# Expert results of a two-layer decoder: from gathers by slot to scatters by row number

## The reference

```python
scores = xf @ Wg
w, idx = jax.lax.top_k(scores, K)            # K = 2 of E = 8 experts
w = jax.nn.softmax(w, axis=-1)
xhat = (xf - mu) * jax.lax.rsqrt(var + EPS)
normed = xhat[None] * gamma[:, None] + beta[:, None]
h = jax.nn.relu(jnp.einsum('end,edf->enf', normed, W1) + b1[:, None])
out = jnp.einsum('enf,efd->end', h, W2) + b2[:, None] + xf[None]
cw = jnp.sum(w[..., None] * jax.nn.one_hot(idx, E, dtype=w.dtype), axis=1)
y = jnp.einsum('ne,end->nd', cw, out)
```

## Time and profile before

| | |
|---|---|
| device time, median of 3 runs | 2757.27 us (2757.04 to 2762.21) |
| the profiled execution's own time | 2763.08 us |
| its span, first to last instruction | 2761.8 us |
| granted TensorE clock, mean over the span | 0.895 |
| PE busy | 2188.1 us, 79% |
| DVE, ACT, POOL busy | 1627.2, 1182.3, 617.8 us |
| scatters ahead of the loop | 748.1 to 791.6 us |
| loop over slots, PE | 795.8 to 1084.4 us |
| from there to the linear attention | 1084.4 to 1146.4 us |
| transfers issued by POOL | 8.39 MB, 0.9% of 16 engines |

### The profile page before, as it was taken

The page is one execution under the profiler, slowest core; times in us unless marked ns, Lnnn a source line. Parts: engine busy times, 40 slices in busy tenths (PEclk is TensorE's granted clock), DMA queues, the critical chain, the costliest instruction groups (busy, mean ns, idle before and its releaser), DMA issues. The chain is left out here.

```text
span 2761.8 us, 41898 instructions
## 1 busy us (share of the span) xinstructions
PE 2188.1 (79%) x15624; PEld 1422.4 (52%) x15694; DVE 1627.2 (59%) x3375; ACT 1182.3 (43%) x2185; POOL 617.8 (22%) x541
## 2 busy tenths in 40 slices
PE   5987589896439997487789999994877786878678
PEld 3554167573427886244345565562555443455534
DVE  5866955467823333566666666625777533777663
ACT  2133845455113332132235555553665433566442
POOL 2110013132153554201110000002221222222152
PEclk9997799897669998688989999996998998899999
DMA  4113124341431111333411101102000001000100
GB/s 136 46 53 92 40 85 143 118 136 47 204 120 40 47 47 51 88 79 79 122 32 33 29 25 37 25 1 91 1 1 1 11 1 61 1 1 1 41 8 24
DMA packets 103780, 151.80 MB, mean 55 GB/s; under 512 B 25188, under 2 KB 84544, under 8 KB 101056
## 3 DMA queue, kind: packets, MB, share of 16 engines
q1 hardware_dynamic: 100512, 140.73, 16.5%
q0 software_dynamic: 3072, 8.39, 0.9%
HBM read 107.07 MB, written 47.98 MB: 56 GB/s over the span
## 5 line engine op out<-in xcount | busy, mean ns | idle before, releaser
L2688 DVE TENSOR_REDUCE xa_max<-psum 128x1 f32<-128x1024 f32 (+1 forms) x256 | 248.4, 988 | 132.5 <-PE psum L2598 131.9
L2769 ACT ACTIVATE xa_work<-psum 128x1024 f32<-128x1024 f32 (+1 forms) x208 | 212.9, 1024 | 188.9 <-PE psum L2621 187.1
L2636 PE MATMUL psum<-xa_work,xa_values 128*33 128x128 f32 (+1 forms) x3328 | 223.9, 277 | 0.0
L2636 PEld LDWEIGHTS psum<-xa_work,xa_values 128*33 128x33 f32 (+1 forms) x3328 | 168.1, 111 | 73.7 <-issue 70.2
L2959 PE MATMUL psum<-wqkv_l,x_hl_l 128*128 128x512 bf16 x538 | 136.9, 400 | 66.2 <-POOL x_hl_l L3219 33.2
L3325 PE MATMUL psum<-h_ch_f,w_f 128*128 128x512 bf16 (+1 forms) x556 | 136.6, 400 | 34.4 <-issue 13.1
L1838 DVE TENSOR_SCALAR moe_raw<-psum,tile_b 128x256 f32<-128x256 f32 x184 | 78.3, 475 | 137.2 <-PE psum L1673 136.1
L994 POOL TENSOR_TENSOR text_q<-text_q 128x512 bf16<-128x512 f32 x64 | 81.8, 1293 | 344.8 <-ACT text_q L1364 344.6
L1919 POOL TENSOR_TENSOR x_ch<-moe_raw,x_ch 128x512 bf16<-128x512 f32 x92 | 105.6, 1158 | 147.1 <-ACT x_ch L1883 145.1
L1673 PE MATMUL psum<-moe_rows,moe_w 128*128 128x256 bf16 x1104 | 131.7, 277 | 3.0 <-POOL moe_rows L1915 3.0
L2621 PE MATMUL psum<-xa_query_rows,xa_key_rows 98*128 98x512 bf16 (+1 forms) x416 | 127.2, 388 | 8.4 <-ACT xa_work L2769 7.7
(11 more groups left out here) (457 smaller groups left out, 4763.5 us busy)
## 6 DMA issues: line engine op xcount, KB each, us to landing
text_q<-in_moe_w SPq DMA_DIRECT2D x64, 256.0 KB, 3.8
experts<-text_q SPq DMA_DIRECT2D x64, 256.0 KB, 3.0
moe_w<-experts SPq DMA_DIRECT2D x16, 1024.0 KB
xa_key_rows<-cross_keys SPq DMA_DIRECT2D x48, 200.1 KB, 3.4
ctx_chunk<-in_ctxT SPq DMA_DIRECT2D x24, 300.0 KB, 3.0
moe_rows<-slots_in SPq DMA_DIRECT2D x23, 256.0 KB, 2.8
slots_out<-moe_rows SPq DMA_DIRECT2D x23, 256.0 KB, 2.2
cross_keys<-xa_k_hl SPq DMA_DIRECT2D x6, 800.5 KB, 3.7
```

What stands on the lines that cost most here:

```text
L2636: ins = pe.matmul(total.ap[a * LANE:a * LANE + VC, c:c + PIECE], t["v"][b][0:rows, kt, first + a, :], exps[0:rows, a, c:c + PIECE], start= ...
L2688: v.tensor_reduce(t["maxes"][n % 2][:, qt * HU + a, part:part + 1], u.wide[:, 0:c1 - c0], AX.X, ALU.max).then_inc(*u.free)
L2769: act.activation(t["exps"][k % EXPS][0:rows], u.wide[0:rows].rearrange("p (m q) -> p m q", q=T), ACT.Exp, scale=1.0 / float(np.sqrt(np.flo ...
```

## The change

Each row of `slots_in` gets a 257th word, an integer: the row of `pairs_out` to which this row's result belongs (k x 2048 + token for a pair, numbers from 4096 on for unused rows). DVE writes it into the tiles before the first 16 scatters (k = 0), and anew, once these have landed, for the other 16 (k = 1); the scatters go in the order k, then tile. The fill now writes zero rows out of on-chip memory and, with a second transfer, 5888 single words. The store of each slot on SP is gone; in its place POOL issues two indirect transfers a slot (`send`), which take `y_out` to `pairs_out` by the numbers that lie in the slot's `x_in` buffer. The load into that buffer therefore also waits for this slot's two sends. Behind the loop, SP loads the results with 8 plain transfers of 512 KB in place of POOL's 32 gathers, and DVE waits once for each pair number and group in place of once for each instruction. Each added wait stands in the diff, cut to its core:

```diff
@@ -1541,11 +1543,19 @@
-def fill_slots(m):
...
-    for a in range(0, SLOTS * SLOT, NTOK):
-        n = min(NTOK, SLOTS * SLOT - a)
-        m.nc.sync.dma_start(m.dram["slots_in"][a:a + n, :], m.dram["x"][0:n, :]).then_inc(*m.slots.filled.up(16))
+def fill_slots(m, s, blank, number):
...
+    g, n = m.nc.gpsimd, SLOTS * SLOT // P
+    g.memset(blank[:], 0.0).then_inc(*s.blank.up())
+    g.tensor_scalar(number[:, 0, :], m.const("ramp")[:, 0:n], float(P), float(PAIRS * NTOK + P - 1), ALU.mult, ALU.add).then_inc(*s.blank.up())
+    g.wait_ge(*s.blank(2))
+    g.tensor_tensor(number[:, 0, :], number[:, 0, :], m.const("left").to_broadcast([P, n]), ALU.subtract).then_inc(*s.blank.up())
+    g.wait_ge(*s.blank(3))
+    g.tensor_copy(number[:, 1, :].bitcast(INT), number[:, 0, :]).then_inc(*s.blank.up())
+    slots = m.dram["slots_in"].rearrange("(n p) c -> p n c", p=P)
+    m.nc.sync.wait_ge(*s.blank(4))
+    m.nc.sync.dma_start(slots[:, :, 0:D], blank[:].unsqueeze(1).to_broadcast([P, n, D])).then_inc(*m.slots.filled.up(16))
+    m.nc.sync.dma_start(slots[:, :, D:ROW], number[:, 1, :].unsqueeze(2), allow_slow_non_contiguous=True).then_inc(*m.slots.filled.up(16))
@@ -1557,25 +1567,26 @@
-                 slot=sb("pair_slot", [P, PAIRS, TILES]), slot_i=sb("pair_slot_i", [P, PAIRS, TILES], mybir.dt.int32),
+                 slot=sb("pair_slot", [P, PAIRS, TILES]), nth=sb("token_number", [P, TILES]), slot_i=sb("pair_slot_i", [P, PAIRS, TILES], mybir.dt.int32),
...
-        raw, rows = sb("moe_raw", [P, 2 * 1024]), sb("moe_rows", [P, TILES, D])
+        raw, rows = sb("moe_raw", [P, 2 * 1024]), sb("moe_rows", [P, TILES, ROW])
...
-        t.update(hat=rows, value=[quarter(raw[:], n) for n in range(2)], act=[quarter(raw[:], 2 + n) for n in range(2)],
-                 x_in=[quarter(flat_rows, n) for n in range(3)], y_out=[quarter(flat_rows, 3 + n) for n in range(2)],
-                 gates=flat_rows[0:NE, 5 * BANK:6 * BANK],
-                 x=[flat_rows[:, (6 + n) * BANK:(7 + n) * BANK].bitcast(BF16).rearrange("p (x h c) -> p x h c", x=2, h=HALVES)
+        t.update(hat=rows[:, :, 0:D], number=rows[:, :, D:ROW].rearrange("p t c -> p (t c)").bitcast(INT), sent=rows, value=[quarter(raw[:], n) for n in range(2)], act=[quarter(raw[:], 2 + n) for n in range(2)],
+                 y_out=[quarter(flat_rows[:, 0:8 * BANK], n) for n in range(2)],
+                 x_in=[flat_rows[:, 5 * BANK + 2 * ROW * n:5 * BANK + 2 * ROW * (n + 1)].rearrange("p (a c) -> p a c", c=ROW) for n in range(3)],
+                 gates=flat_rows[0:NE, 4 * BANK:5 * BANK],
+                 x=[flat_rows[:, (2 + n) * BANK:(3 + n) * BANK].bitcast(BF16).rearrange("p (x h c) -> p x h c", x=2, h=HALVES)
...
-                      "in_high in_low h_high h_low stored0 stored1 combined")
-        moved = m.signals("scattered back0 back1 back2 back3 back4 back5 back6 back7", first=70)
+                      "in_high in_low h_high h_low combined")
+        moved = m.signals("scattered0 scattered1 scattered2 scattered3 sent0 sent1 numbered back0 back1 back2 back3", first=70)
@@ -1614,23 +1629,28 @@
         sp.dma_start(t["w2"][:, e], dram["experts_2"][e]).then_inc(*s.w_loaded.up(16))
 
     slots_in = dram["slots_in"].rearrange("(j a p) d -> j p a d", a=2, p=P)
-    slots_out = dram["slots_out"].rearrange("(j a p) d -> j p a d", a=2, p=P)
 
     def load(j):
         if j > 2:
             sp.wait_ge(*use["turn", j - 3].full)
+            sp.wait_ge(*sent(moved, j - 3)(16 * 2 * ((j - 3) // 2 + 1)))
         sp.dma_start(t["x_in"][j % 3], slots_in[j]).then_inc(*x_loaded(s, j).up(16))
 
-    sp.wait_ge(*moved.scattered(16 * PAIRS * TILES))
+    for g in range(B):
+        sp.wait_ge(*scattered(moved, g)(16 * PAIRS * TPB))
     load(0)
     load(1)
     for step in plan:
         kind, j = step[:2]
         if kind == "turn" and j + 2 < SLOTS:
             load(j + 2)
-        elif kind == "second":
-            sp.wait_ge(*use[step].done)
-            sp.dma_start(slots_out[j], t["y_out"][j % 2]).then_inc(*stored(s, j).up(16))
+    for j in range(SLOTS - 2, SLOTS):
+        sp.wait_ge(*sent(moved, j)(16 * 2 * (j // 2 + 1)))
+    sp.wait_ge(*use["second", SLOTS - 1].full)
+    pairs = dram["pairs_out"][0:PAIRS * NTOK, :].rearrange("(k t p) d -> p k t d", k=PAIRS, p=P)
+    for g in range(B):
+        for k in range(PAIRS):
+            sp.dma_start(t["back"][:, k, TPB * g:TPB * (g + 1), :], pairs[:, k, TPB * g:TPB * (g + 1), :]).then_inc(*came_back(moved, g).up(16))
 
 
 def experts_pe(m, s, t, use, plan):
@@ -1709,6 +1729,12 @@
+    v.tensor_scalar(t["nth"][:], m.const("ramp")[:, 0:TILES], float(P), float(P - 1), ALU.mult, ALU.add).then_inc(*s.v_step.up())
+    v.wait_ge(*s.v_step.now())
+    v.tensor_tensor(t["nth"][:], t["nth"][:], m.const("left").to_broadcast([P, TILES]), ALU.subtract).then_inc(*s.v_step.up())
+    v.wait_ge(*s.v_step.now())
+    v.tensor_copy(t["number"], t["nth"][:]).then_inc(*moved.numbered.up())
+    v.tensor_scalar(t["nth"][:], t["nth"][:], float(NTOK), None, ALU.add).then_inc(*s.v_step.up())
@@ -1800,6 +1826,10 @@
+    for g in range(B):
+        v.wait_ge(*scattered(moved, g)(16 * TPB))
+        v.tensor_copy(t["number"][:, TPB * g:TPB * (g + 1)], t["nth"][:, TPB * g:TPB * (g + 1)]).then_inc(*moved.numbered.up())
@@ -1844,20 +1874,22 @@
             v.scalar_tensor_tensor(m.x_tok[:, tile, :], m.x_tok[:, tile, :], gsum[:, tile:tile + 1], u.ap[:, 0:D],
                                    ALU.mult, ALU.add).then_inc(*u.free)
     for g in range(B):
+        v.wait_ge(*came_back(moved, g)(16 * PAIRS))
         for tile in group(g):
-            x = m.x_tok[:, tile, :]
             v.wait_ge(*use["residual", tile].done)
-            v.wait_ge(*came_back(moved, tile)(16 * 2 * PAIRS))
-            for k in range(PAIRS):
-                v.scalar_tensor_tensor(x, t["back"][:, k, tile, :], t["weight"][:, k, tile:tile + 1], x, ALU.mult, ALU.add).then_inc(*s.combined.up())
-                v.wait_ge(*s.combined.now())
+        for k in range(PAIRS):
+            for tile in group(g):
+                x = m.x_tok[:, tile, :]
+                ins = v.scalar_tensor_tensor(x, t["back"][:, k, tile, :], t["weight"][:, k, tile:tile + 1], x, ALU.mult, ALU.add)
+            ins.then_inc(*s.combined.up())
+            v.wait_ge(*s.combined.now())
         norm_dve(m, s, g + 2, m.x_tok, m.x_tok, group(g))
         if g:
             bitnet_channels_dve(m, use, g - 1)
     bitnet_channels_dve(m, use, B - 1)
 
 
-def experts_act(m, s, t, use, plan):
+def experts_act(m, s, moved, t, use, plan):
     act = m.nc.scalar
     act.wait_ge(*s.variance(TILES))
     act.activation(m.std[:], m.mv[:, :, 1], ACT.Sqrt, bias=m.eps[:, 1:2]).then_inc(*s.deviation.up())
@@ -1883,7 +1915,7 @@
-                act.wait_ge(*stored(s, j)(16 * (j // 2)))
+                act.wait_ge(*sent(moved, j)(16 * 2 * (j // 2)))
@@ -1900,29 +1932,41 @@
     bitnet_channels_act(m, use, B - 1)
 
 
-def experts_pool(m, s, moved, t):
+def experts_pool(m, s, moved, t, use):
     g = m.nc.gpsimd
     g.wait_ge(*s.addressed(1))
-    g.wait_ge(*m.slots.filled(16 * 3))
-    for tile in range(TILES):
-        g.wait_ge(*s.normed(tile + 1))
-        for k in range(PAIRS):
+    g.wait_ge(*m.slots.filled(32))
+    for k in range(PAIRS):
+        for tile in range(TILES):
+            if k == 0:
+                g.wait_ge(*s.normed(tile + 1))
+            g.wait_ge(*moved.numbered(1 + k * (1 + tile // TPB)))
             to = bass.IndirectOffsetOnAxis(ap=t["slot_i"][:, k, tile:tile + 1], axis=0)
-            g.indirect_dma_start(m.dram["slots_in"], to, t["hat"][:, tile, :], None).then_inc(*moved.scattered.up(16))
-    for j in range(SLOTS):
+            g.indirect_dma_start(m.dram["slots_in"], to, t["sent"][:, tile, :], None).then_inc(*scattered(moved, tile // TPB).up(16))
+
+    def inputs(j):
         x = t["x"][j % 2]
         g.wait_ge(*s.in_high(j + 1))
         g.tensor_tensor(x[:, 1], t["value"][j % 2], x[:, 0], ALU.subtract).then_inc(*s.in_low.up())
+
+    def send(j):
+
+        g.wait_ge(*use["second", j].done)
+        for a in range(2):
+            where = bass.IndirectOffsetOnAxis(ap=t["x_in"][j % 3][:, a, D:ROW].bitcast(INT), axis=0)
+            g.indirect_dma_start(m.dram["pairs_out"], where, t["y_out"][j % 2][:, a, :], None).then_inc(*sent(moved, j).up(16))
+
+    inputs(0)
+    for j in range(SLOTS):
         for q in range(4):
             n, hidden, f = 4 * j + q, t["hidden"][j % 2], slice(2 * q, 2 * q + 2)
             g.wait_ge(*s.h_high(n + 1))
             g.tensor_tensor(hidden[:, 1, f, :], t["act"][n % 2], hidden[:, 0, f, :], ALU.subtract).then_inc(*s.h_low.up())
-    for j in range(SLOTS - 2, SLOTS):
-        g.wait_ge(*stored(s, j)(16 * (j // 2 + 1)))
-    for tile in range(TILES):
-        for k in range(PAIRS):
-            where = bass.IndirectOffsetOnAxis(ap=t["slot_i"][:, k, tile:tile + 1], axis=0)
```

(26 more changed lines are left out.)

## The result

| | before | after |
|---|---|---|
| median, us | 2757.52 (2757.04 to 2762.21, 4 runs) | 2883.20 (2876.07 to 2886.74, 4 runs) |
| ratio, 95% interval | | 1.0449 (1.0426 to 1.0471) |
| profiled execution | 2763.08 | 2882.63 |
| its span | 2761.8 | 2881.3 |
| PE, from the loop's first transposes to the end of its last second | 795.8 to 1084.4: 288.6 | 797.0 to 1223.7: 426.8 |

The change makes the kernel slower by 126 us; the forecast was 115 (2872, range 2826 to 2925). In the two traces the loop grows by 138 us, the stretch behind it shrinks by 19, the time up to the loop grows by 1.2, and the rest of the kernel is as it was.

A forecast was written before the change was run, and what follows sets the result against it. PE alone was taken to bound the loop, busy 11.11 of 11.17 us a slot. Behind the loop -17.6 us and inside it +132 gave +114, stated against the median before as 2872 us, range 2826 to 2925.

The forecast's parts named there:

- Part 1: Behind the loop: plain loads replace gathers and DVE waits less often, so the stage ends sooner; -17.6 us, bounds -14 and -20.
- Part 2: In the loop: SP's load waits for sends, so PE stands still 5.0 us before each turn, 20 times; +132 us with clock loss.
- The clock: In the loop: PE's matmuls run slower behind each stop, losing 1.6 us a stop, bounds 0 and 2.5.
- the signs: What would show it: period 17 to 18.5 us, PE idle about 5 us, clock near 0.9, slots 0 to 2 unchanged.
- Part 3: POOL, ACT and SP in the loop: two indirect transfers add 2.5 us a slot on POOL, at no cost.
- the rival of the blocked send: In the loop: DVE blocks a send each slot, 2.2 us more, 44 us in all; 2916 us, chance 0.06.
- Part 4: Ahead of the loop: scatters keep their 1.27 us pace, fill and DVE's added work are hidden; 0, up to 20 us above.
- The sum: Whole kernel: -17.6 + 132 = +114 us, stated against the median before as 2872 us; chance 0.72.
- no loss of clock: In the loop: PE stops before each turn but loses no clock behind the stop; 2840 us, chance 0.12.
- the load in time: At the turn: sends and load finish within PE's other work, leaving only the gain behind the loop; 2740 us, chance 0.05.

The follow-up runs named there:

- e1: The changed kernel, but POOL copies each slot's row numbers out of x_in and the load waits for that copy, not the sends; 0.9942 of before.
- e2: The changed kernel with four x_in buffers in place of three, the load waiting for the sends of slot j - 4; 0.9946 of before.
- e4: The changed kernel with two extra POOL subtractions of about 0.65 us each ahead of each slot's two sends; 1.0571 of before.
- e6: The kernel before, without sends, with the load of slot j + 3 issued behind the landing of slot j's store; 1.0288 of before, 79 us.
- e3: The changed kernel with 18 matmuls of unused output on PE before it waits for the load of each slot from 3 on; 1.0305 of before.

## Why the prediction was right, point by point

- **Part 1, behind the loop**: -17.6 forecast, -19.1 in the trace. The loads land sooner (DVE starts 10.3 us after PE's end, 11.1 forecast) and eight sums take 3.38 us, not 3.54.
- **Part 2, the stop**: 5.0 us forecast, 4.8 measured (4.7 to 5.0), from slot 3 on and 20 times. By terms: copy 0.7 as forecast; POOL's start 0.27 us after the copy, forecast 0.7, which came from a start behind a transfer; between the starts of the two sends 1.30; from the second one to PE's transposes 963.40 - 958.23 = 5.17, forecast 2.43 + 2.72 = 5.15. The transfer of 257 words a row is no slower. The part of the gap that PE fills itself is 2.6 us (955.97 to 958.6), not 2.8. e1, e2 and e4 show that this one wait is all but some 3 us of the loss in the loop; e6 shows that a late load alone, without any send, makes a loss of the same kind.
- **The clock**: 1.6 us a stop forecast, 2.0 by e3. This is the largest error of size in the sum, 8 us; the stop, forecast 4 us too long over the 20 slots, hides half of it, which is luck. The granted clock over the loop was 0.85, where the signs named 0.9. The two rows it was taken from lost 1.7 in matmuls alone; here the transposes at the front run slow too (1.12 against 0.63 us). That this makes the difference is likely but not isolated.
- **Part 3**: POOL's added 2.5 us a slot are hidden: e1 runs at 11.1 us a slot with them. Slots 0 to 2, said to stay as they were, took 3 us more up to the first stop (42.2 against 39.0 us); in e6, which has no sends, it was 41.0, so at most about 1 us of it can come from them. The sends took 0.97 to 0.99 us, all 46 of them, beside DVE's L1868. So the rival of the blocked send fell. The prediction's reason for it, that L1868 reads PSUM, fits but is not isolated: L1868 is also short, 0.44 us.
- **Part 4**: 0 forecast, +1.2 in the trace. The fill and DVE's waits are hidden as described (DVE ready at 777.0, forecast 774); the scatters come every 1.27 to 1.28 us.
- **The sum**: 20 x 6.8 - 19.1 + 1.2 = +118, against +119.6 between the two profiled executions. The medians lie 125.7 apart. The difference is that the profiled execution before was itself 5.6 us over its median and the one after was not; the forecast was set against the median, so it carried the trace's difference and missed these 6.
- The rivals: no loss of clock (2840) fell with e3; the load in time (2740) is what e1 and e2 give once the wait is moved, 0.9942 and 0.9946 of before.

## What to carry to other kernels

When something new lives in the buffer of a prefetch ring, ask when its last reader is done, not when its first is: here the rows were read at the start of a slot's work and the row numbers at its end, and the prefetch lost its lead. Compare the chain from that last read to the use of the reloaded buffer with the work the bound engine has in between; if it is longer, the difference comes back in every turn of the loop, and on PE the clock's loss on top. Copy the few words out, or add one buffer: either turned a loss of 4.5% into a gain of 0.6%. In e2 the same wait stayed and cost nothing, because one slot more of lead covered it.

## What the runs showed of the hardware that was not expected

- A transfer of 5888 pieces of 4 bytes held SP's queue for 16.1 us, while one of 5888 KB in rows of 1 KB ahead of it was issued in 0.39 us and landed after 27.6. Here it was hidden.
- An indirect transfer on POOL took 3.15 to 3.17 us in the kernel before, in the one after and in every run that left the product whole, always beside the one DVE instruction of 2.8 us with two operands in SBUF, and 1.28 once that instruction was cut into eight. In the kernel before and in the one after, the transfer ended 0.84 and 0.86 us after the product did (758.81 to 759.65, 759.64 to 760.50). The Trainium skill (SBUF — State Buffer, Terms) describes a pair of ports that one engine holds for a whole instruction, and these rows agree with it; that the ports are the reason, no run here isolates. DVE's eight pieces together took 3.31 us, longer than the whole; what went is the length of a single instruction.
- Gaps of PE of 2.8 to 3.7 us between dense work (e6) cost clock in some slots and none in others: with gaps of 2.85 to 3.0 us periods ran from 14.0 us at a clock of 1.00 to 16.9 us. On average they cost about 1 us each; gaps of 4.8 us, in the kernel after, cost 2.0. What decides it from slot to slot stays open.
